# The maximum in front of a softmax: from one GpSimd subtraction to the bias of sixteen ScalarE exponentials, and query's low part one place earlier

## What is computed

```
q = x @ Wq + bq;  k = ctx @ Wk + bk;  v = ctx @ Wv + bv
scores = einsum('bkgld,bksd->bkgls', q, k) * scale      # scale = 32 ** -0.5
scores = scores + mask
attn = softmax(scores, axis=-1)
out = einsum('bkgls,bksd->bkgld', attn, v)
out = out @ Wo + bo;  x = layer_norm(out + x) * gamma + beta
```

## Time and profile before

| | us |
|---|---|
| median of 3 runs | 1802.25 (1800.71 to 1804.18) |
| the profiled execution | 1800.33 |
| its span, first to last instruction | 1798.5 |
| TensorE busy | 1735.8 (97%), mean granted clock 0.992 |
| VectorE busy | 1103.3 (61%) |
| GpSimd busy | 1098.5 (61%) |
| ScalarE busy | 584.0 (32%) |

### The profile page before, as it was taken

How to read it: one execution, slowest core, us unless ns; L and a number is a source line. 1 busy time by engine, 2 the same in 40 slices (tenths; PEclk the granted TensorE clock), 3 DMA queues, 4 the chain that set the end, 5 groups by cost and what they waited for, 6 DMA issues and landing times.

```text
span 1798.5 us, 22557 instructions
## 1 busy us (share of the span) xinstructions
PE 1735.8 (97%) x8577; PEld 1443.9 (80%) x8577; DVE 1103.3 (61%) x1073; ACT 584.0 (32%) x667; POOL 1098.5 (61%) x607
## 2 busy tenths in 40 slices
PE   6999999999999799999999998999999999999998
PEld 5788878788888688888888877788888888888887
DVE  6888888888878444544444555446644664466442
ACT  4444444434444433333333322213311331133110
POOL 3677777777787756565655576536543664466431
PEclk9999999999999999999999999999999999999999
DMA  8433332333225557676777754454844474456332
GB/s 219 113 82 81 95 80 74 86 77 76 72 74 161 164 180 242 206 242 209 241 234 234 264 169 134 154 173 134 247 140 165 140 217 147 164 153 198 117 119 103
DMA packets 272367, 278.02 MB, mean 155 GB/s; under 512 B 63226, under 2 KB 223108, under 8 KB 272260
## 3 DMA queue, kind: packets, MB, share of 16 engines
q1 hardware_dynamic: 270068, 274.48, 49.3%
q10 hardware_dynamic: 2192, 2.10, 0.4%
HBM read 174.77 MB, written 101.71 MB: 154 GB/s over the span
## 4 chain that ended last, share of the span: by engine, by line
PE 64%; DVE 15%; issue 8%; POOL 6%; ACT 5%; DMA 1%; SPq 0%; POOLq 0%; DVEq 0%; ACTq 0%
PE ps L53 20%; PE ps L55 20%; PE ps L54 20%; DVE small L1057 3%; DVE pr L1077 3%; ACT pr L827 3%; DVE pT0r L1090 2%; DVE pT1r L1090 2%; DVE xT1r L988 2%; ACT ot L821 2%; PE ps L687 1%; DVE xT0r L988 1%; PE ps L695 1%; DMA wv0r<-in_L_xattn_Wv_dram 1%; PE ps L662 1%
## 5 line engine op out<-in xcount | busy, mean ns | idle before, releaser
L1363 POOL TENSOR_TENSOR x2Tl<-x2r,x2Th 128x1024 fp32r<-128x1024 f32 x32 | 76.8, 2400 | 291.0 <-ACT x2Th L929 291.0
L1163 DVE STREAM_TRANSPOSE x2r<-xd 128x1024 f32<-128x1024 f32 x32 | 68.7, 2147 | 210.8 <-PE ps L55 210.8
L1299 POOL TENSOR_TENSOR pr<-pr,small 128x1024 f32<-128x1024 f32 x64 | 122.8, 1919 | 99.0 <-DVE small L1083 99.0
L929 ACT CAST x2Th<-x2r 128x1024 fp32r<-128x1024 f32 x32 | 33.7, 1052 | 375.7 <-DVE x2r L1163 375.7
L1294 POOL TENSOR_TENSOR pr<-pr,small 128x1024 f32<-128x1024 f32 x64 | 123.9, 1935 | 25.5 <-DVE small L1061 25.5
L1057 DVE TENSOR_REDUCE small<-pr 128x16 f32<-128x1024 f32 x64 | 78.0, 1219 | 78.7 <-ACT pr L827 78.7
L1314 POOL TENSOR_TENSOR xb<-xb,bo 128x1024 f32<-128x1024 f32 x32 | 78.2, 2443 | 78.4 <-DMA xb<-in_x_dram 78.4
L1133 DVE TENSOR_TENSOR y<-ps,xb 128x512 f32<-128x512 f32 x64 | 44.0, 687 | 116.6 <-PE ps L55 113.5
L1328 POOL TENSOR_TENSOR y<-y,bet 128x1024 f32<-128x1024 f32 x32 | 77.7, 2428 | 52.3 <-DVE y L1102 52.3
L53 PE MATMUL ps<-wo0h,oc1l 128*128 128x512 f32 x256 | 103.4, 404 | 4.3 <-DVE y L1133 4.3
L53 PE MATMUL ps<-wo0h,oc0l 128*128 128x512 f32 x256 | 103.0, 402 | 1.7 <-DVE wo0l L1012 1.7
(11 more groups left out here) (371 smaller groups left out, 5492.8 us busy)
## 6 DMA issues: line engine op xcount, KB each, us to landing
o_scratch<-ot SPq DMA_DIRECT2D x256, 64.0 KB, 1.8
ocr<-o_scratch SPq DMA_DIRECT2D x16, 1024.0 KB, 7.9
xb<-in_x_dram SPq DMA_DIRECT2D x32, 512.0 KB, 6.7
x_scratch<-y SPq DMA_DIRECT2D x32, 512.0 KB, 5.2
a_scratch<-ost SPq DMA_DIRECT2D x64, 256.0 KB, 3.5
b_scratch<-ost SPq DMA_DIRECT2D x64, 256.0 KB, 4.6
xd<-x_scratch SPq DMA_DIRECT2D x128, 128.0 KB, 2.9
raw<-b_scratch SPq DMA_DIRECT2D x64, 256.0 KB, 5.6
```

The source lines that it names most:

```text
L1163: nc.vector.transpose(x2r[:].rearrange("p k (t j) -> p t k j", t=TPB), xd[:].rearrange("p t (i k) -> p t k i", k=KT)).then_inc(x2_turned, 1)
L1299: nc.gpsimd.tensor_tensor(heads(v), heads(v), mx.unsqueeze(2).to_broadcast([P, TPB * GRP, KEYS]), ALU.subtract)\
L1363: nc.gpsimd.tensor_tensor(x2T[1][:], x2r[:], f32(x2T[0][:]), ALU.subtract).then_inc(x2_lo, 1)
```

## The change

It has three parts. (1) The subtraction on GpSimd and its semaphore go. In its place each exponential takes minus the maximum as its bias, and since a bias is one value per partition, and a unit has 16 maxima per partition, the exponential becomes 16 instructions of 64 keys; only the last signals. (2) ScalarE adds the bias and can't subtract it. So keys are scaled by -SCALE0, the mask is subtracted and not added, the minimum is taken (which is minus the maximum), and the exponential has scale -1. (3) On VectorE q_lo of unit u stands in front of the turn of u-2, and not behind it. The maximum of v now waits until the exponential of v-1 is done (`exped`) and not `centered`.

```diff
-                    act.wait_ge(centered, v + 1)
-                    e = pr[v % 2][:].rearrange("p j m s -> p (j m s)")
-                    nc.scalar.activation(e, e, ACT.Exp).then_inc(exped, 1)
+                    act.wait_ge(maxed, v + 1)
+                    e = pr[v % 2][:].rearrange("p j m s -> p (j m) s")
+                    for i in range(TPB * GRP):
+                        last = nc.scalar.activation(e[:, i], e[:, i], ACT.Exp, scale=-1.0, bias=mx[:, i:i + 1])
+                    last.then_inc(exped, 1)
...
-                nc.vector.tensor_scalar(kf[:, h], V[h][:, :CTX], bk[:, h:h + 1], SCALE0, ALU.add, ALU.mult).then_inc(kfull, 1)
+                nc.vector.tensor_scalar(kf[:, h], V[h][:, :CTX], bk[:, h:h + 1], -SCALE0, ALU.add, ALU.mult).then_inc(kfull, 1)
...
-                                            mask[t % 2][:].unsqueeze(2).to_broadcast([P, TPB, GRP, KEYS]), ALU.add)\
+                                            mask[t % 2][:].unsqueeze(2).to_broadcast([P, TPB, GRP, KEYS]), ALU.subtract)\
...
-                    after(dve, centered, v)
-                    nc.vector.tensor_reduce(mx, p[:].rearrange("p j m s -> p (j m) s"), AX_X, ALU.max).then_inc(maxed, 1)
+                    after(dve, exped, v)
+                    nc.vector.tensor_reduce(mx, p[:].rearrange("p j m s -> p (j m) s"), AX_X, ALU.min).then_inc(maxed, 1)
...
-                if 1 <= u <= UNITS:
-                    v = u - 1
-                    pool.wait_ge(maxed, v + 1)
-                    nc.gpsimd.tensor_tensor(heads(v), heads(v), mx.unsqueeze(2).to_broadcast([P, TPB * GRP, KEYS]), ALU.subtract)\
-                        .then_inc(centered, 1)
```

More of the change, by code:

```diff
@@ L178, in program @@
          vfull, v_hi, v_lo, kv_st, vv_st, wq_hi, wq_lo, x_turned, x_hi, x_lo, q_done, q_hi, q_lo, zeroed, mask_ld, scores,
-         s_read, maxed, centered, exped, summed, recips, probs, p_turned, p_hi, p_lo, pv, o_ev) = (sem(n) for n in (
+         s_read, maxed, exped, summed, recips, probs, p_turned, p_hi, p_lo, pv, o_ev) = (sem(n) for n in (
              "ctx_ld kv_ld0 kv_ld1 b_ld b_turned b_done ones ctx_t ctx_hi ctx_lo kv_hi kv_lo k_done v_done kfull k_hi k_lo vfull v_hi "
-             "v_lo kv_st vv_st wq_hi wq_lo x_turned x_hi x_lo q_done q_hi q_lo zeroed mask_ld scores s_read maxed centered "
+             "v_lo kv_st vv_st wq_hi wq_lo x_turned x_hi x_lo q_done q_hi q_lo zeroed mask_ld scores s_read maxed "
              "exped summed recips probs p_turned p_hi p_lo pv o_ev").split())
@@ L1078, in slot @@
                                             S[v % 2].rearrange("p (m j s) -> p m j s", m=TPB, j=GRP),
-                                            mask[t % 2][:].unsqueeze(2).to_broadcast([P, TPB, GRP, KEYS]), ALU.add)\
+                                            mask[t % 2][:].unsqueeze(2).to_broadcast([P, TPB, GRP, KEYS]), ALU.subtract)\
                         .then_inc(s_read, 1)
                     dve.wait_ge(s_read, v + 1)
-                    after(dve, centered, v)
-                    nc.vector.tensor_reduce(mx, p[:].rearrange("p j m s -> p (j m) s"), AX_X, ALU.max).then_inc(maxed, 1)
+                    after(dve, exped, v)
+                    nc.vector.tensor_reduce(mx, p[:].rearrange("p j m s -> p (j m) s"), AX_X, ALU.min).then_inc(maxed, 1)
                 if u == UNITS:
                     split_wo(7)
+                if u < UNITS:
+                    dve.wait_ge(q_hi, u + 1)
+                    nc.vector.scalar_tensor_tensor(out=qs[u % 2][1][:], in0=Q[u % 2].rearrange("p (n m) -> p m n", m=TPB), scalar=bq[:, u % KT:u % KT + 1],
+                                                   in1=f32(qs[u % 2][0][:]), op0=ALU.add, op1=ALU.subtract).then_inc(q_lo, 1)
                 if 2 <= u < UNITS + 2:
@@ L1091, in slot @@
                                         pr[v % 2][:].rearrange("p j m (b i) -> p (j m) b i", b=2)).then_inc(p_turned, 1)
[L1092 to L1095, removed]
                 if u in (UNITS - 2, UNITS - 1):
```

## The result

| | before | after |
|---|---|---|
| median of the four runs | 1801.9 us | 2008.66 us (2007.63 to 2013.73) |
| ratio to before | | 1.115, 95% interval 1.114 to 1.117 |
| span of the profiled execution | 1798.5 | 2007.1 |
| first to last start of the sum | 50.2 to 601.1 | 51.9 to 811.2 |
| mean from sum to sum, 63 slots | 8.74 | 12.05 |

The changed kernel is slower by 208.6 us between the two profiled spans. All of it lies in the attention stage of layer one.

The account below looks back on a forecast made before the run. The prediction took the loop between VectorE and ScalarE as the bound, with TensorE just behind. Its terms summed to +208.5 us, 2008.8, or 2010.7 by the median; it said 2010, range 1975 to 2060.

Parts of the forecast that it names:

- the loop between VectorE and ScalarE: Attention stage: turn, p_hi, ot, exponential, sum, reciprocal, mask, maximum, turn; claimed to set the pace, 8.55 us a slot on average.
- GpSimd's subtraction off the path: Attention stage: removing 64 GpSimd instructions was to gain nothing on the path; the exponential had waited for it once, 1.1 us.
- Sixteen exponentials: ScalarE, each attention slot: 3.97 us from first exponential to sum in place of 1.09, +2.88 us a slot.
- The two ways: Two estimates, from ScalarE trace rows, of the exponentials' start-to-start distance: 0.235 us and 0.197 us; 0.24 was taken.
- the forecast 0.6 us: Margin in a slot with a turn of x by which q_hi was to be ready before VectorE reaches q_lo.
- the low-clock rival: Attention stage, all 64 slots: idle pieces lower TensorE's clock, its 8.3 us become 16.5 and bound it; 2285 us, chance 0.06.
- first sum: Start of the stage: exponential 0 no longer waits 1.1 us for the subtraction, its sum comes 2.88 later: +1.8 us.
- 54 slots up to the last with a turn of x: Sums from 50.2 to 521.39: 54 x 3.51 = 189.5, less 2 for stalls of the turn: +187.5 us.
- 6 slots without one: From 521.39 to 569.46, 48.1 us; by the loop 6 x 11.06 = 66.4: +18.3 us.
- 3 last slots: From 569.46 to 601.12, 31.7 us; 11.06 twice and 11.7 with a split of Wo make 33.8: +2.2 us.
- last turn: Last turn of the probabilities, at 605.93: 3.45 us after its sum's start in place of 4.81: -1.35 us.
- The four stalls for GpSimd: The turn's waits for GpSimd's product, 0.4 us each in 4 slots, were to go: 2 us less.

## Why the prediction was right

The forecast of 2010 us stands against 2008.66, and the range held it. Point by point:

- **What bounds the kernel**: the loop between VectorE and ScalarE. Shown four times: by what q_lo in the loop costs, by what ot out of it gives, by the extra matmuls that cost only 2.3 us over 63 slots, and by the sixteen moved out of it. One sign of it I had wrong: VectorE's wait for the exponential was to grow from 1.3 to about 3.6 us a slot, and it is 4.9. VectorE's own work is unchanged, so its wait had to take the whole growth of 3.5, which the slots in the sum did have.
- **GpSimd's subtraction off the path**: shown, no difference without it in the order of before.
- **Sixteen exponentials**: 3.97 us from the first to the sum, as worked out; 0.240 us from start to start against 0.24. The two ways had given 0.235 and 0.197; the one whose rows read and write SBUF was right. The part for the pointer, 92 ns from the earlier trace rows, was confirmed by itself.
- **q_lo**: 0.66 us in the loop instead of 0.63, since it takes 0.742 us there where it took 0.709. From the first sum on it never waited for q_hi; in the slot shown above q_hi ended at 302.74 and q_lo started at 303.35, the forecast 0.6 us.
- **TensorE**: idle, with a dip of the clock in each slot with a turn of x, as the low-clock rival had it, but off the path. I had said 2 and 4 us of waits for q_lo; they are about 1 and 4. The busy share of the stage is 78%, not 70, which is 9.4 us a slot instead of 8.3, most likely because a matmul at low clock counts as busy for longer. The idle time held the dip by less than I said: behind a dip the projection wasn't ready 5 us ahead of q_hi, but 0.50 us behind ScalarE's arrival (q_hi at 311.14). What was left was the 2.6 us between the end of that q_hi and q_lo at 314.43.
- **The sum, term by term** (between the profiled spans):

| term | predicted | measured |
|---|---|---|
| first sum | +1.8 | +1.7 |
| 54 slots up to the last with a turn of x | +187.5 | +185.9 |
| 6 slots without one | +18.3 | +18.4 |
| 3 last slots | +2.2 | +4.1 |
| last turn | -1.35 | -1.3 |
| together | +208.5 | +208.8 |

The one term that was clearly off is that of the last slots. The split of Wo in the slot behind the last unit, which I took at 1.2 us, lasted 2.97. VectorE, and GpSimd at the same time:

```profile
801.16 2.34 POOL L1311 TENSOR_TENSOR xb<-xb,bo 128x1024 f32<-128x1024 f32 x1
...
801.61 2.97 DVE L1014 TENSOR_TENSOR wo0l<-wo0r,wo0h 128x1024 fp32r<-128x1024 f32 x1
804.50 1.23 DVE L1096 STREAM_TRANSPOSE pT0r<-pr 128x1024 f32<-128x1024 f32 x1
...
811.16 1.22 DVE L1059 TENSOR_REDUCE small<-pr 128x16 f32<-128x1024 f32 x1 [4.12 <-ACT pr L828]
```

GpSimd's xb ended at 803.50, and the split 1.08 us later, as if it had run only then. In the kernel before the same pair of engines met the other way round:

```profile
594.30 1.22 DVE L1012 TENSOR_TENSOR wo0l<-wo0r,wo0h 128x1024 fp32r<-128x1024 f32 x1
594.47 2.82 POOL L1299 TENSOR_TENSOR pr<-pr,small 128x1024 f32<-128x1024 f32 x1 [0.57 <-DVE small L1083]
```

There the split started first and took 1.22, and the subtraction, 1.92 us on average, took 2.82. With the subtraction gone, xb follows GpSimd's product at once and gets in front of the split. It was the same with the sixteen alone, where this split took 3.02; in the kernel before without the subtraction xb waited for a transfer, the split came first, and it took 1.22. So by the order of GpSimd's queue it is the missing subtraction that cost 1.75 us here, where the prediction had its removal at nothing; no run has the sixteen with the subtraction still in its place.

That the total came out so close is in part luck: this error of 1.9 us is offset by 1.6 in the 54 slots. There one of the first, which split Wq, grew by only 2.8 us, and of the others those with a turn of x grew by 3.45 and those without by 3.53, where 3.51 was forecast for both. The four stalls for GpSimd went, as forecast.

Two numbers of the prediction outside its sum are slips. By its own 9.5 us for 10 ns, a distance of 0.197 us gives 1970 and not 1965. And the rule that gives it 5.65 us for the sixteen is 0.353 a piece; less an overlap of 0.093 that is 0.26 and not 0.24. The forecast rests on neither.

## What to carry to other kernels
- When one engine is 97% busy, look for a closed loop of others before calling it the bound: follow the starts through one period, and ask which of them waits for the busy engine. If none does, the loop sets the pace, and each microsecond put into it costs one microsecond a round, whatever is freed elsewhere.
- What a wait is worth isn't decided where it is seen. TensorE's wait for q_lo was an effect of the loop, and serving it sooner from inside the loop made it longer.
- Splitting an instruction into sixteen multiplies its fixed part and adds that of a pointer operand (here 0.185 of the 0.240 us a piece). And before an instruction is moved out of one loop, sum up what its new neighbours queue in front of it on every engine, or the next loop is built by the move.

## What the runs showed of the hardware
- A ScalarE instruction of 64 columns costs 0.148 us from start to start without a pointer operand and 0.240 with one: 0.092 us for the pointer, the same as from instructions of 1024 columns.
- In the changed kernel the granted clock fell to 0.50 during waits of about 4 us of TensorE's and stayed up through waits of about 1 us. It came back to 1.00 with TensorE at work. That cost nothing in the changed kernel, and time where the dip lay on the chain (0.43 us a matmul instead of 0.23). 12 more matmuls a slot brought the stage's mean from 0.90 to 0.98.
- VectorE's low parts of 1024 columns and GpSimd's instructions of 1024 columns didn't run side by side in the pairs looked at: the one that started second ended about its own time after the first. VectorE's split of Wo took 1.22 us when it was first and 2.97 behind xb. The low part of x took 1.36 behind GpSimd's subtraction (303.75 to 305.65) and 1.18 in the changed kernel. GpSimd's low part took 3.01 behind that split of x and 2.38 in the changed kernel. VectorE's sum kept its 1.220 us with GpSimd busy 76 or 53 of 100 us.
